# The experts' opening dealt into the last causal batch, weights cast midway, and the last batch routed one batch ahead

## Chip, cores and metric

The kernel runs on one core of one Trainium2 chip. The metric is the time of the device in microseconds (us). Several runs of a kernel give a median, and one more run is taken with the hardware profiler.

## What is computed

The input `x` has 8 batches of 512 positions with 512 channels. The reference applies three blocks, one after the other:

```python
x = x + tanh(g_xattn) * cross_attention(layernorm(x), ctx)     # pass A
y = layernorm(x)
y = y + latent_attention(rmsnorm(y, w_ln1))                    # pass B, causal, 16 heads
y = y + moe(rmsnorm(y, w_ln2))                                 # pass C
x = x + tanh(g_ffn) * y

def moe(x):
    shared = (silu(x @ sWg) * (x @ sWu)) @ sWd                 # one expert, all 4096 rows
    p = softmax(x @ Wgate + expert_bias)                       # 8 experts, the best 2 per row
    top_p, top_i = top_k(p, 2);  top_p /= sum(top_p)
    routed = sum_e comb[:, e] * ((silu(x @ Wg[e]) * (x @ Wu[e])) @ Wd[e])
    return shared + routed
```

The kernel computes `routed` only for the rows that chose an expert: it sorts them into 71 blocks of 128 rows, each with one expert.

## The kernel before

Every matrix product of pass C runs as three f16 products, from a high half (`_hi`, a cast) and a low half (`_lo`, the rest) of each operand. ACT writes the high halves, DVE or POOL the low ones.

**Order.** Each engine runs its own list of instructions in the order in which the Python code emits them, and they meet through semaphores. Passes A and B are generators with 64 steps for each batch, and `run_both` (L1615) deals B's first steps between A's last ones. B ends with an end body, which computes the last output projection. Its output `z` is stored to `z_all` by SP (L1111), POOL clears A's semaphores (L1218), and the block ends in a barrier (L1626). Pass C (`pass_c`, L1669) then begins with a block and memory of its own.

**Pass C, dense part.** It works on batches b = 0 to 7, and a body b does the shared expert of batch b and prepares batch b+1:

- SP loads `z` of a batch (1 MB, `load_z`, L1810) into one of four slots, and the f32 weights of one routed expert per body into a single stage (`gu_stage`, 1 MB in two transfers, L1819; `d_stage`, 0.5 MB, L1824). In a body's list stand, in this order, `load_z(b+3)` from body 1 to body 4, `up_weights(b+1)`, `down_weights(b+1)`. `load_z(b+3)` waits until the slot is free, which is when the store of batch b-1 has landed.
- POOL stores a finished batch with an accumulating transfer (`add_to_output`, L1878), so that of batch b-1 at the start of its body b. It also writes the routing records into a table with indirect transfers (`scatter`, L1901, 64 in all), takes the root for the norm (`rms`), and makes a low half (L1882).
- ACT squares and normalises the rows of batch b+2 (L2000, L2005), casts transposed rows (`high`, L1992), takes a tanh (`squash`, L2027), casts the hidden layer (`hidden_high`, L2033), scales by the gate (L2010) and casts the staged weights (`weights`, L2015 and L2017).
- DVE makes low halves (L2121, L2127, L2132), chooses the experts of a row (`choose`), works out its place in the table (`shares`, `read_ranks`, `place_rows`), makes the hidden layer (`activate`, L2277, L2280), and adds the gate and residual (`finish_rows`, L2290).
- PE, in a body: `up(b)` with 12 products to a chunk, four chunks (L2433 to L2435); four turns of batch b+1 (L2393); `route(b+1)` (L2403); `down(b)` (L2444 to L2446); `rank(b+1)` (L2416 to L2421), which ends the body. The last row of L2421 is used below as the mark of a body's end.

**Routed part.** After body 7 DVE lays out the blocks (`lay_starts`, `lay_blocks`). SP waits until all records are scattered, and loads the entries of each block (L1855). POOL gathers the rows of a block (L1948), ACT scales them, PE turns them (`x_turn`, L2485) and does up and down with that block's expert. POOL adds the result to the output in an indirect transfer. The gather of block 3 waits for all stores of the dense part. PE waits for the last casts and for the last dense output ahead of the loop.

## Time and profile before

| | |
|---|---|
| median of 3 runs | 2330.65 us (2325.38 to 2334.54) |
| the profiled run | 2325.74 us |
| its span | 2324.0 us, granted clock 0.964 |
| PE busy | 2103.3 us, 91% |
| DVE, ACT, POOL busy | 64%, 51%, 59% |

The times of the trace are us from the start of the span. Passes A and B take the stretch to about 1757, the dense part of C that from 1757 to 1963, and the routed blocks the rest. A row of the timeline gives the start, the length, the engine, the line and the operation, with the tile written ahead of the arrow, and in brackets how long the engine had been idle and what released it. A row marked x8 stands for eight instructions, and its time is that of the whole group. SPq rows are the moments at which SP issues a transfer, not the transfers.

### The profile page before, as it was taken

The numbers are of one execution on the slowest core, as the hardware profiler recorded it, in microseconds if no ns is written. First come the engines' busy times: TensorE is split into PE (matmuls) and PEld (weight loads), VectorE is DVE, ScalarE is ACT, GpSimd is POOL, SyncE is SP. The second block draws the span as 40 slices with busy tenths as digits, with TensorE's granted clock in tenths as the row PEclk, the third lists the DMA queues.
The fourth block names the chain that finished last, engine by engine and source line by source line (L and its number), as shares of the span: only waits on it lengthen the run. The fifth ranks groups of instructions, "written<-read, shape, count | busy, mean of one in ns | idle before, by whom it ended". The sixth has DMA issues, their size and how long they took to land. (4 is left out here: it accounts for less than half of the span.)

```text
span 2324.0 us, 43302 instructions
## 1 busy us (share of the span) xinstructions
PE 2103.3 (91%) x12568; PEld 958.9 (41%) x12569; DVE 1489.1 (64%) x4180; ACT 1180.0 (51%) x2319; POOL 1374.2 (59%) x1450
## 2 busy tenths in 40 slices
PE   2899999999999977799999999999984897899997
PEld 1333333333333312344444444544432443455554
DVE  3688888888888874466566565655544678344443
ACT  3355555555555544345545455554544673455554
POOL 4267776776776765255656565665661575455554
PEclk7999999999999987899999999999997998999999
DMA  5513323232332222534535354353514676666665
GB/s 161 168 55 110 101 85 103 81 115 73 107 97 92 78 98 86 170 115 139 159 118 153 117 163 134 114 174 98 155 49 159 120 156 126 114 116 112 115 109 91
DMA packets 227973, 272.15 MB, mean 117 GB/s; under 512 B 40152, under 2 KB 165964, under 8 KB 227508
## 3 DMA queue, kind: packets, MB, share of 16 engines
q1 hardware_dynamic: 197324, 212.76, 30.3%
q0 software_dynamic: 22752, 47.86, 12.1%
q10 hardware_dynamic: 7704, 9.20, 1.2%
q8 instruction: 92, 1.51, 0.3%
q14 instruction: 101, 0.83, 0.1%
HBM read 161.82 MB, written 86.54 MB: 107 GB/s over the span
## 5 line engine op out<-in xcount | busy, mean ns | idle before, releaser
L501 ACT ACTIVATE a_pt<-a_bank 128x512 f32<-128x512 f32 x512 | 305.6, 597 | 370.2 <-DVE a_bank L608 367.3
L1439 DVE CUSTOM_DVE_ANT_0 b_bank<-b_bank,b_tri 128x256 f32<-128x256 f32 (+3 forms) x512 | 253.2, 497 | 296.0 <-PE b_bank L1579 291.8
L619 DVE CUSTOM_DVE_ANT_0 a_bank<-a_bank,a_strip 128x512 f32<-128x512 f32 x512 | 353.2, 691 | 4.6 <-PE a_bank L762 3.9
L1192 POOL TENSOR_TENSOR b_acc<-b_acc,b_pt 128x256 f32<-128x256 f32 (+2 forms) x384 | 279.2, 749 | 84.2 <-ACT b_pt L1305 73.3
L411 POOL TENSOR_TENSOR a_acc<-a_acc,a_pt 128x512 f32<-128x512 f32 x256 | 317.5, 1271 | 16.2 <-ACT a_pt L501 15.7
L608 DVE TENSOR_TENSOR a_bank<-a_bank,a_band 128x256 f32<-128x256 f32 (+1 forms) x512 | 205.6, 402 | 129.7 <-PE a_bank L749 128.5
L1305 ACT ACTIVATE b_pt<-b_bank 128x256 f32<-128x256 f32 (+2 forms) x384 | 143.7, 383 | 187.1 <-PE b_bank L1563 171.1
L749 PE MATMUL a_bank<-a_q_stack,a_k_stack 128*128 128x512 f16 x512 | 199.2, 390 | 22.9 <-ACT a_pt L501 13.9
L762 PE MATMUL a_bank<-a_k_stack,a_q_stack 97*128 97x512 f16 x512 | 196.4, 384 | 3.6 <-DVE a_low L619 3.5
L1964 POOL DMA_INDIRECT out_dram<-c_z,c_to_row x71 | 112.5, 1585 | 133.8 <-DMA out_dram<-c_z,c_to_row 97.6
L1578 PE MATMUL b_bank<-b_k_stack,b_q_stack 96*128 96x256 f16 (+3 forms) x512 | 154.6, 302 | 16.0 <-DVE b_low L1439 8.7
L1561 PE MATMUL b_bank<-b_q_stack,b_k_stack 96*128 96x256 f16 (+3 forms) x512 | 156.4, 306 | 9.5 <-ACT b_pt L1305 5.6
L408 POOL TENSOR_TENSOR a_acc<-a_pt 128x512 f32<-128x512 f32 x128 | 159.9, 1269 | 4.9 <-ACT a_pt L501 4.9
L429 POOL TENSOR_TENSOR a_o_un<-a_o_un,a_den 128x512 f32<-128x512 f32 x32 | 41.3, 1292 | 204.4 <-DVE a_den L572 204.4
L1563 PE MATMUL b_bank<-b_q_stack,b_k_stack 97*128 97x256 f16 (+3 forms) x512 | 154.2, 301 | 0.0
L1579 PE MATMUL b_bank<-b_k_stack,b_q_stack 96*128 96x256 f16 (+3 forms) x512 | 153.2, 300 | 0.0
L777 PE MATMUL a_bank<-a_pt,a_v 128*32 128x512 f32 x1024 | 142.4, 629 | 1.1 <-ACT a_pt L501 1.1
L1207 POOL TENSOR_TENSOR b_o_un<-b_o_un,b_den 128x512 f32<-128x512 f32 x32 | 40.8, 1276 | 157.1 <-DVE b_den L1395 147.3
L749 PEld LDWEIGHTS a_bank<-a_q_stack,a_k_stack 128*128 128x128 f16 x512 | 49.5, 97 | 183.0 <-ACT a_pt L501 91.1
L1305 ACT ACTIVATE b_acc<-b_bank 128x512 f32<-128x512 f32 x128 | 74.7, 596 | 92.4 <-PE b_bank L1563 86.4
L1562 PE MATMUL b_bank<-b_hidden,b_far 128*128 128x128 bf16 x512 | 113.0, 221 | 0.0
L2343 DVE TENSOR_TENSOR c_xt_lo<-c_bank,c_xt_hi 128x512 f16<-128x512 f32 x71 | 49.0, 691 | 94.3 <-ACT c_xt_hi L2082 94.3
(338 smaller groups left out, 5352.7 us busy)
## 6 DMA issues: line engine op xcount, KB each, us to landing
b_q_stack<-qk_rows SPq DMA_DIRECT2D x192, 128.0 KB, 2.6
a_q_stack<-qk_rows SPq DMA_DIRECT2D x96, 128.0 KB
a_k_stack<-qk_rows SPq DMA_DIRECT2D x96, 128.0 KB
b_k_stack<-qk_rows SPq DMA_DIRECT2D x96, 128.0 KB, 2.6
a_sums<-in_x SPq DMA_DIRECT2D x34, 256.0 KB, 3.2
qk_rows<-a_qk_hi SPq DMA_DIRECT2D x64, 128.0 KB, 1.7
qk_rows<-a_qk_lo SPq DMA_DIRECT2D x64, 128.0 KB, 1.8
out_dram<-a_sums SPq DMA_DIRECT2D x32, 256.0 KB, 2.0
```

Source lines behind the costliest of these rows:

```text
L408: nc.gpsimd.tensor_tensor(acc[:, hh, :], pt[:, (n - HG) % SLOTS, :], mine, ALU.add).then_inc(pooled, 1)
L411: nc.gpsimd.tensor_tensor(acc[:, hh, :], acc[:, hh, :], mine, ALU.add).then_inc(pooled, 1)
L501: nc.scalar.activation(pt[:, n % SLOTS, :], st_bank[n % 2][:], ACT.Exp).then_inc(exped, 1)
L608: nc.vector.tensor_tensor(st_bank[n % 2][:, c0:c1], st_bank[n % 2][:, c0:c1], band[:, h, at:at + c1 - c0], ALU.add).then_inc(biased, 1)
L619: nc.vector.tensor_tensor_reduce(out=max_bank[step % 2][:], in0=max_bank[step % 2][:], in1=strip[:, g * HG + hh, at:at + S], scale=-1.0, s ...
L749: mm(st_bank[n % 2][:], k_stack[:, h, j * P:(j + 1) * P], q_stack[:, h, :], start=True, stop=True).then_inc(scored, 1)
L762: mm(max_bank[step % 2][:], q_stack[0:MASK + 1, h, i * P:(i + 1) * P], k_stack[0:MASK + 1, h, :], start=True, stop=True).then_inc(maxed, 1)
L1192: nc.gpsimd.tensor_tensor(sums_of, sums_of, probs(n), ALU.add).then_inc(pooled, 1)
L1305: nc.scalar.activation(probs(n), st_bank[n % 2][:, 0:w], ACT.Exp).then_inc(exped, 1)
L1439: nc.vector.tensor_tensor_reduce(out=max_bank[step % 2][:, 0:w], in0=max_bank[step % 2][:, 0:w], in1=tri[:, at:at + w], scale=-1.0, scalar ...
L1561: mm(o, k_stack[0][0:LOW, h, j * P:(j + 1) * P], q_stack[0][0:LOW, h, j * P:], start=True, stop=False)
L1578: mm(o, q_stack[0][0:LOW, h, c], k_stack[0][0:LOW, h, 0:w], start=True, stop=False)
```

## The change

Lines of the changed kernel are those of its own file.

1. **One program.** `run_all` takes the place of `run_both` and of C's own block. C's passes become generators too. C's opening (all that PE, ACT, DVE and POOL do ahead of body 0, with `up(0, 0, 0)`) is cut into 90 steps, and these are dealt between B's steps from step 38 of B's last batch. `inputs_used` (B's last query and key rows are consumed) and `all_used` (B's last output is evicted) are the waits that stand in place of the barrier.
2. **Memory.** C's tiles and PSUM banks are laid over what B has finished with. The shared expert's halves get tiles of their own (`own_gu_hi` and others), and C uses B's identity matrix.
3. **SP.** C's constants, z(0), the shared expert's weights, z(1) and the blank table are issued in B's last batch, ahead of its last four stores. z(2) and z(3) follow after B's end.
4. **Semaphores.** POOL clears A's semaphores at the start of B's third batch instead of at B's end.
5. **Weights cast midway.** ACT's cast of the next expert's up weights moves from the end of body b to its middle, between `high(b+1, 1)` and `high(b+1, 2)`; the cast of the down weights to behind `hidden_high(b, 1)`. DVE makes the low halves of the same expert in the same body, where it made them one body later before.
6. **Last batch ahead.** Batch 7 is routed within body 6. POOL has 3 of the 32 row tiles to scatter in body 7, where it had 4. DVE lays out the blocks at the start of body 7, and takes the first three `from_row` there. PE turns block 0 ahead of its waits for casts and output.

The core of the diff:

```diff
 JOIN = 46
+NEXT_JOIN = 38
+OPENING = 2 * UNITS - NEXT_JOIN
@@ pass B, SP body
+                if kind == "last":
+                    yield
@@ run_both -> run_all
+    def chained(second, third):
+        for at, _ in enumerate(second):
+            if at >= next_joined:
+                next(third)
+            yield
+        yield from third
@@ pass C, SP
-            sp.dma_start(table, blank_rows).then_inc(blanked, 16)
-            load_z(0)
+            prior.inputs_used(sp)
...
+            load_z(0)
             sp.dma_start(r_stage[:], ...)
             up_weights(0)
             down_weights(0)
             load_z(1)
+            sp.dma_start(table, blank_rows).then_inc(blanked, 16)
+            yield
+            prior.all_used(sp)
             load_z(2)
+            sp.wait_ge(prior.z1_stored, 64 * B + 16)
             load_z(3)
             for b in range(B):
...
                 if b and b + 3 < B:
                     load_z(b + 3)
                 up_weights(b + 1)
                 down_weights(b + 1)
@@ pass C, ACT
-            square(0)
...
+            for s in range(OPENING):
+                if s < NT:
+                    square(0, (s,))
...
+                if 8 <= s < 8 + NT:
+                    normalise(0, (s - 8,))
+                if 12 <= s < 12 + NK:
+                    up_weights(0, (s - 12,))
...
+                yield
+            prior.all_used(act)
             for b in range(B):
                 more = b + 1 < B
                 squash(b, 0)
                 if more:
                     high(b + 1, 0)
                     high(b + 1, 1)
-                    scale_gate(b + 1, range(0, 2))
+                up_weights(b + 1)
+                if more:
                     high(b + 1, 2)
                     high(b + 1, 3)
                 hidden_high(b, 0)
                 if b + 2 < B:
                     square(b + 2)
                 squash(b, 1)
                 if more:
-                    scale_gate(b + 1, range(2, 4))
+                    scale_gate(b + 1, range(0, 2))
+                if b + 2 == B:
+                    exponential(b + 1)
                 hidden_high(b, 1)
+                down_weights(b + 1)
                 if b + 2 < B:
                     normalise(b + 2)
+                    exponential(b + 1)
                 if more:
-                    exponential(b + 1)
-                weights(b + 1)
+                    scale_gate(b + 1, range(2, 4))
@@ pass C, PE
+            for s in range(OPENING):
+                if 13 <= s < 13 + NT:
+                    turn(0, s - 13)
+                if s == 40:
+                    route(0)
+                    up(0, 0, 0)
+                yield
+            prior.all_used(pe)
             for b in range(B):
-                up(b, 0, 0)
-                if b == 0:
+                more, early = b + 1 < B, b + 2 == B
+                if b:
+                    up(b, 0, 0)
+                else:
                     rank(0)
...
                 up(b, 1, 0)
+                if early:
+                    route(b + 1)
                 up(b, 1, 1)
-                if more:
+                if more and not early:
                     route(b + 1)
                 for t in range(NT - 1):
                     down(b, t, (0,))
+                if early:
+                    rank(b + 1)
```

On ACT, in the body of batch 1 of the dense part (`c_th` is `squash`, `c_xt_hi` is `high`, `c_h_hi` is `hidden_high`, the squares write `c_xn,c_squares`), the order before was:

```order
L2027 ACTIVATE c_th<-c_bank 128x512 [waits c_half_done,c_up_done]
L1992 ACTIVATE c_xt_hi<-c_bank 128x4x128 [waits c_logits_done,c_up_done,c_turned] x2
L2010 ACTIVATE c_z<-c_z,c_gate 128x512 [waits c_xn_ready]
L2010 ACTIVATE c_z<-c_z,c_gate 128x512
L1992 ACTIVATE c_xt_hi<-c_bank 128x4x128 [waits c_logits_done,c_up_done,c_turned] x2
L2033 ACTIVATE c_h_hi<-c_hid 128x512 [waits c_downed,c_hidden]
L2000 ACTIVATE c_xn,c_squares<-c_z 128x512 [waits c_turned,c_z_loaded0]
```

and it is now, with the body's second half:

```order
L2099 ACTIVATE c_th<-c_bank 128x512 [waits c_half_done,c_up_done]
L2062 ACTIVATE c_xt_hi<-c_bank 128x4x128 [waits c_logits_done,c_up_done,c_turned] x2
L2085 ACTIVATE c_gu_hi<-c_gu_stage,c_wn 128x512 [waits c_gu_loaded]
L2085 ACTIVATE c_gu_hi<-c_gu_stage,c_wn 128x512 x3
L2062 ACTIVATE c_xt_hi<-c_bank 128x4x128 [waits c_logits_done,c_up_done,c_turned] x2
L2105 ACTIVATE c_h_hi<-c_hid 128x512 [waits c_downed,c_hidden]
L2070 ACTIVATE c_xn,c_squares<-c_z 128x512 [waits c_turned,c_z_loaded3]
L2070 ACTIVATE c_xn,c_squares<-c_z 128x512 x3
L2099 ACTIVATE c_th<-c_bank 128x512 [waits c_half_done,c_up_done]
```

The cast of the staged weights, which waits for their load, now stands between the two pairs of `high`; before, it stood behind the body's last instructions.

On SP, the loads of the dense part's bodies 0 to 2 in the changed kernel (L1867 is `load_z`, L1876 the up weights, L1881 the down weights, L1904 a part of the table):

```order
L1876 DMA c_gu_stage<-in_Wg 128x4x256 [waits c_w_split]
L1876 DMA c_gu_stage<-in_Wu 128x4x256
L1881 DMA c_d_stage<-in_Wd 128x2x512 [waits c_w_split]
L1904 DMA table<-c_blank 128x8x4 [waits a_m_stacked1,a_m_stacked2]
L1867 DMA c_z<-z_all 128x4x512 [waits c_out_stored0]
L1876 DMA c_gu_stage<-in_Wg 128x4x256 [waits c_w_split]
L1876 DMA c_gu_stage<-in_Wu 128x4x256
L1881 DMA c_d_stage<-in_Wd 128x2x512 [waits c_w_split]
L1867 DMA c_z<-z_all 128x4x512 [waits c_out_stored1]
L1876 DMA c_gu_stage<-in_Wg 128x4x256 [waits c_w_split]
```

Nothing moved here: the same rows, with the waits of the same semaphores, stand in the same order in the kernel before.

On PE, at the end of pass B, the last rows of its output projection and the first of pass C before:

```order
L1483 MATMUL b_bank<-b_wo_hi,b_o_hi 128x512 [waits b_o_lo_done]
L1484 MATMUL b_bank<-b_wo_lo,b_o_hi 128x512
L1485 MATMUL b_bank<-b_wo_hi,b_o_lo 128x512
L1626 UNCONDITIONAL_BRANCH
L2382 UNCONDITIONAL_BRANCH [waits barrier_Pool_Activation_PE_DVE_SP_release]
L2393 MATMUL c_bank<-c_idn,c_xn 128x128 [waits c_xn_ready,c_const_set,c_const_loaded]
```

and now, from the end of C's first chunk of `up` (L2539 to L2541) and from the end of the output projection (L1498 to L1500) on:

```order
L2539 MATMUL c_bank<-c_xt_hi,c_own_gu_hi 128x512
L2540 MATMUL c_bank<-c_xt_lo,c_own_gu_hi 128x512
L2541 MATMUL c_bank<-c_xt_hi,c_own_gu_lo 128x512
L1498 MATMUL b_bank<-b_wo_hi,b_o_hi 128x512 [waits b_o_lo_done]
...
L1500 MATMUL b_bank<-b_wo_hi,b_o_lo 128x512
L2522 MATMUL c_bank<-c_chosen,c_before_p 128x32 [waits a_normed,c_const_set,b_left_dve]
```

The turns, `route(0)` and the first `up` stand ahead of B's last chains, and `rank(0)` is the first of C's rows behind them.

## Rows read from the trace of the kernel before

**Rows 1.** The page: busy tenths of PE in 40 slices of the span.

```profile
PE   2899999999999977799999999999984897899997
```

**Rows 2.** Busy us by stretch: PE, PEld, DVE, ACT, POOL; clock, DMA share, GB/s.

```profile
1690.00:1741.50 51.50, 44.41 (x352) 19.96 (x350) 20.08 (x67) 26.23 (x62) 32.68 (x44) 0.97 0.15 50
...
1757.00:1789.00 32.00, 9.86 (x82) 6.57 (x83) 9.71 (x36) 19.29 (x44) 4.93 (x19) 0.57 0.77 262
...
1812.50:1904.50 92.00, 80.58 (x581) 42.37 (x579) 68.17 (x209) 60.92 (x120) 60.41 (x65) 0.94 0.80 157
1904.50:1943.50 39.00, 37.75 (x295) 20.40 (x293) 34.62 (x105) 23.87 (x45) 29.58 (x32) 1.00 0.76 136
```

**Rows 3.** Timeline, all engines: from B's last product to C's first rank.

```profile
1755.00 0.38 PE L1485 MATMUL b_bank<-b_wo_hi,b_o_lo 128*128 128x512 f16 x1
...
1766.03 0.63 ACT L2000 ACTIVATE c_xn<-c_z 128x512 f32<-128x512 f32 x1 [19.55 <-DMA c_z<-z_all]
...
1770.97 1.94 PE L2393 MATMUL c_bank<-c_idn,c_xn 128*128 128x128 f32 x8 [15.59 <-ACT c_xn L2005]
...
1788.96 0.24 PE L2421 MATMUL c_bank<-c_chosen,c_ones 128*128 128x8 f16 x4
```

**Rows 4.** Timeline of PE: ends of bodies 0, 1, 2 and 6.

```profile
1812.48 0.24 PE L2421 MATMUL c_bank<-c_chosen,c_ones 128*128 128x8 f16 x4
...
1831.78 0.24 PE L2421 MATMUL c_bank<-c_chosen,c_ones 128*128 128x8 f16 x4
...
1859.75 0.24 PE L2421 MATMUL c_bank<-c_chosen,c_ones 128*128 128x8 f16 x4
...
1943.47 0.24 PE L2421 MATMUL c_bank<-c_chosen,c_ones 128*128 128x8 f16 x4
```

**Rows 5.** Timeline, bodies 1 to 4: stores, SP's next loads, ACT's casts of them.

```profile
1813.24 1.41 POOL L1878 DMA_DIRECT2D out_dram<-c_z  x1 [4.57 <-DVE c_z L2290]
...
1827.24 0.37 SPq L1810 DMA_DIRECT2D c_z<-z_all  x1
...
1838.54 1.46 POOL L1878 DMA_DIRECT2D out_dram<-c_z  x1
...
1849.93 0.37 SPq L1810 DMA_DIRECT2D c_z<-z_all  x1
...
1850.64 0.37 SPq L1819 DMA_DIRECT2D c_gu_stage<-in_Wg  x1
...
1859.19 2.56 ACT L2015 ACTIVATE c_gu_hi<-c_gu_stage,c_wn 128x512 f16<-128x512 f32 x4 [1.59 <-DMA c_gu_stage<-in_Wu]
...
1873.75 0.51 SPq L1819 DMA_DIRECT2D c_gu_stage<-in_Wg  x1
...
1884.17 2.56 ACT L2015 ACTIVATE c_gu_hi<-c_gu_stage,c_wn 128x512 f16<-128x512 f32 x4 [7.26 <-DMA c_gu_stage<-in_Wu]
```

**Rows 6.** SP's waits by cause, 1757 to 1960: total us, times, longest.

```profile
SPq L1810 <- DMA out_dram<-c_z: 46.5, 3, 19.4
```

**Rows 7.** Transfers: number, size, median us from issue to landing.

```profile
out_dram<-c_z POOLq DMA_DIRECT2D x8, 1024.0 KB, 11.2
...
c_gu_stage<-in_Wu SPq DMA_DIRECT2D x8, 512.0 KB, 6.9
```

**Rows 8.** Timeline: a stall of PE in body 2; second tanh and end of body 3.

```profile
1843.74 1.94 PE L2393 MATMUL c_bank<-c_idn,c_xn 128*128 128x128 f32 x8 [5.65 <-DVE c_xt_lo L2121]
...
1870.64 0.57 ACT L2027 ACTIVATE c_th<-c_bank 128x512 f32<-128x512 f32 x1
...
1879.06 0.24 PE L2421 MATMUL c_bank<-c_chosen,c_ones 128*128 128x8 f16 x4
```

**Rows 9.** Timeline behind body 7: first turn, gather of block 3, its turn.

```profile
1976.68 1.97 PE L2485 MATMUL c_bank<-c_idn,c_z 128*128 128x128 f32 x8 [13.24 <-ACT c_z L2077]
...
1985.72 1.06 POOL L1948 DMA_INDIRECT c_z<-z_all,c_from_row  x1 [9.05 <-DMA out_dram<-c_z]
...
1992.14 0.60 PE L2485 MATMUL c_bank<-c_idn,c_z 128*128 128x128 f32 x4
```

429 lines of the change are left out of this document (254 added, 175 removed).

## The prediction

> **What bounds the kernel now.** I read the page first: PE is busy nine tenths of the span and has one long dip near three quarters of it, and one short dip after that [rows 1]. Any gain or loss lies there. The windows then cut that part into stages [rows 2]. In the tail of pass B (1690 to 1741.5) PE is busy 44.41 of 51.5 us beside ACT's 26.23 and POOL's 32.68. In C's opening (1757 to 1789) it is busy 9.86 of 32, at a granted clock of 0.57, while ACT works 19.29. Bodies 1 to 4 of the dense part (1812.5 to 1904.5) take 92 us, with PE busy 80.58; bodies 5 and 6 take 39, with PE busy 37.75. A body without a disturbance is thus 19.5 us long, and PE's products set it.
>
> The timeline shows what the opening costs: the last output product is at 1755.00, ACT's first square at 1766.03, after 19.55 us idle for `z` to come back from memory, the first turn at 1770.97, and `rank(0)` ends the opening at 1788.96 [rows 3]. Bodies 0, 1 and 2 then end at 1812.48, 1831.78 and 1859.75: 23.5, 19.3 and 28.0 us [rows 4].
>
> Last I followed the weights. In bodies 1 to 4 SP issues `load_z(b+3)`, and behind it the weights for the next cast. SP's wait for the slot, that is for POOL's accumulating store, is the cause of 46.5 us of SP's idle time [rows 6]. The store of body 1 is issued at 1813.24 and SP goes on at 1827.24, 14.0 us later; in body 2 it is 1838.54 and 1849.93, 11.4 us [rows 5]. Then the weights are issued, and ACT's cast of them starts 8.5 us later (1850.64 to 1859.19), in the next body 10.4 us later (1873.75 to 1884.17), both times after a wait for that load [rows 5]. So the weights of body 2 are cast at 1859.19, when PE has all but finished body 2 (1859.75). In the kernel before this lateness is nearly free, since the cast is the last thing on ACT's list for that body, and what is cast is used only in the routed part.
>
> **The change, part by part.** I sum against the profiled run, 2325.74 us, which lies 4.9 us below the median of three.
>
> *Join: -24.* What is removed is the way from B's last product to `rank(0)`, 1755.0 to 1789.0, 34 us [rows 3]. Back come two things. First, `route(0)` and the first `up` must still run on PE, some 3.8 us (an estimate: 48 narrow and 12 wide products, the wide ones 0.38 us long with about half of it overlapped [rows 3]); they stand ahead of B's last output chain, in a tail where PE is idle 7.1 of 51.5 us [rows 2], so I count half of it, 2. Second, B's tail grows. ACT gets nearly all of the 19.29 us that it works in the opening [rows 2] added to the tail, where it had 25.3 us free in 51.5; POOL gets the two norm roots. ACT and PE wait for each other there at each step, so free time is not fully usable. Below it costs 0, if all fits between; above 12, if 60% of ACT's work lengthens the tail. I take 7, nearer to the upper half because ACT would be 88% busy (45.5 of 51.5). `rank(0)` then comes near 1765: 24 saved, between 18 and 31.
>
> *Early loads, memory, semaphores: 0.* SP's loads go out in the last batch, where the DMA share is 0.15 [rows 2], and POOL's 64 clears move to a place where POOL waits for others. If a load should be late for the opening, it costs what the join gains, and that lies in its range.
>
> *Body 0: +2.5.* z(2), z(3) and the first expert's weights, 3 MB, can only start after B's last store; the cast now stands in the middle of body 0. With some 2 us until the store has landed, 10 for the loads (the slower of [rows 5] is 10.4) and 14 or 15 from the cast to the body's end (next paragraph) it takes 26 us, and took 23.5 [rows 3, 4].
>
> *Cast in the middle, bodies 1 to 4: +64.* This adds a wait to ACT, and its list goes on behind that wait: `high(b+1, 2)` and `high(b+1, 3)`, without which PE can't `route`; then `hidden_high(b, 0)`, without which PE can't `down`; then the squares, the second tanh, the second `hidden_high`. PE, DVE and POOL all stop there. SP's order has not been changed: `load_z(b+3)`, which waits for the store of batch b-1, stands ahead of the weights for this cast. And that store is only issued after body b-1 has ended. So within one body there is now a chain with nothing to hide it: end of body b-1, store, `z` load issued, weights loaded, cast, second half of the body. Its pieces:
>
> - end of the body to store: 0.8 us in body 1 (1812.48 to 1813.24), 6.8 in body 2, where POOL still has scatters queued (1831.78 to 1838.54) [rows 4, 5]; I take 2 each for bodies 3 and 4, together 11.6;
> - store to SP's next issue: 11.4 (14.0 in body 1, whose store ran beside other loads) [rows 5], four times 45.6;
> - from there to the issue of the weights 0.7, and to the cast 9.0, between the 8.5 and 10.4 of [rows 5]: 38.8;
> - cast 2.56 [rows 5], then two `high`, one `hidden_high` and four squares, seven operations of the size of one of the cast's four (0.6 each, 4.2), so 6.7 until the second tanh; from there to the end of the body 8.4 (1870.64 to 1879.06 in body 3) [rows 8]: 15.1, four times 60.4.
>
> Together 156.4, where the four took 92.0: +64. The lower bound takes the median landings, 11.2 and 6.9 [rows 7], stores issued at once and 13 for the last piece: 4 x 32.3 = 129, +37. For the upper bound, PE stands still some 15 us in each body. In the trace a PE that had stood for 15.59 us was granted 0.57 over the stretch [rows 2, 3], nearer to the lower of its two levels (1.2 of 2.4 GHz). Then the fifteen last products take twice as long, some 3 us more a body, and with loads of 10.4 the sum is 174, +82.
>
> What the row shows of the store is 11.2 us from issue to landing for 1 MB [rows 7]. The Trainium skill, page "DMA: Bandwidth & Descriptors", section "Anatomy of one DMA — SWDGE (gpsimd) path", gives a fit of 2.0 us and bytes over 436e3 per us, by which 1 MB would be an estimated 4.4 us; four bodies would then be 27 us shorter and the whole near 2333. The trace doesn't agree for this accumulating store, and the row decides. The same section says that a DMA engine does not wait on semaphores, and that the wait is on the issuing sequencer; SP's 46.5 us [rows 6] agree.
>
> *Bodies 5 and 6: +2.* No `z` is loaded there, so the weights come a body ahead: 0. Batch 7's choice and places run within body 6, where DVE already works 34.62 of 39 in two bodies [rows 2]; I give 2, between 0 and 4.
>
> *Last batch ahead: -10.* From body 6's end to the turn of block 3 it took 48.7 us (1943.47 to 1992.14) [rows 4, 9]. With the table laid out early, the first gathers no longer lie behind the dense part's end, and PE's 13.24 us of idle ahead of its first turn go. Next is the gather of block 3, which waits for the last store: body 7's products, 19.5 as in bodies 5 and 6 [rows 2], finishing 1, store 11.2 [rows 7], gather to turn 6.4 (1985.72 to 1992.14) [rows 9], together 38.1. The bounds are -6, if the entries come late, and -14, if the store is 3 or 4 us shorter.
>
> Sum: -24 + 2.5 + 64 + 2 - 10 = +34.5, so 2360 us.
>
> **Rivals.**
>
> *Hidden after all: faster.* The weights land before ACT comes to the cast, because the store is issued earlier or SP's wait is met sooner than I think. Bodies 1 to 4 then take 4 x 19.3 = 77 [rows 4], 15 less than now, and body 0 its +2.5: 2325.7 - 24 + 2.5 - 15 + 2 - 10 = 2281. Against it: even in the kernel before, ACT waited for this load at the body's very end [rows 5]. This side begins when the four bodies take under 28.6 us on average: gains and losses are level at (92.0 + 24 - 2.5 - 2 + 10) / 4 = 30.4 us each. I give 0.12.
>
> *Level: within 0.5%.* The chain is there, but its transfers are shorter, since they run more by themselves (the same bytes at a DMA share of 0.80 in 92 us [rows 2] would be some 0.5 in 150). With 9.5 for the store, 6.9 for the load [rows 7], 13 for the tail and stores issued after 1 us, a body is 30.8 us: 2327. Against it: the store of body 2 had no `z` or up weights beside it and still took 11.4 [rows 5]. 0.14. The shorter store that the Trainium skill's fit gives would fall on this side too.
>
> *Join lost as well: slower still.* ACT's added work lengthens B's tail by its whole 19 us and the opening's own chain is stretched; -24 becomes -10, and the time 2374. For it: the 88% on ACT. Against it: of the idle time in the opening, 15.59 us is PE's wait for a load, a norm and ACT [rows 3], which is gone either way. 0.10.
>
> *My forecast*, 2342 to 2370: 0.64.
>
> **How the numbers follow.** About 0.5% is what a measurement of this kernel can tell from no change, here 2319 to 2342 around the median. Slower takes the forecast and the lost join: 0.74; the same 0.14; faster 0.12. The predicted time is the forecast's, 2360. The range of 8 in 10 runs from 2332, inside the level case, to 2380, the upper bound of the chain with a good join; it leaves out the faster case, part of the level one, and little above.
>
> **What the profile of the changed kernel would show.** Join right: the first `up` products ahead of B's last output products, no gap of 15 us between the two passes, `rank(0)` near 1765. Chain right: ACT's cast of `c_gu_hi` waits for the transfer into `c_gu_stage` some 10 to 18 us in each of four bodies, PE idles ahead of `route` or `down`, its granted clock falls in these bodies, and they are 36 to 42 us long; SP's wait on the store still stands ahead. Last batch right: the turn of block 3 about 38 us after body 6's end. Wrong would be: casts of bodies 1 to 4 with short waits and ends 19 to 25 us apart (faster), or a B tail that ends much after 1765.

## The result and the profile after

The changed kernel takes 2378.98 us (median of four runs, 2375.21 to 2381.74), beside 2328.30 for the kernel before: 1.0213 times as long, 95% interval 1.0186 to 1.0240. Its profiled run is one of 2375.21 us with a span of 2373.4, so 49.4 us of span came on top; the forecast was 34.5. The page of the profile shows where: PE's dip near three quarters of [rows 1], one deep slice, has become a trough over four slices, and in three of them the granted clock is at 7 tenths (in one before).

```profile
PE   2899999999999968899999999999976658899997
PEclk8999999999999978999999999999987779899999
```

The windows of the changed kernel, in the columns of [rows 2]: the tail of pass B with the opening dealt into it, the stretch from there to `rank(0)`, bodies 1 to 4, and about bodies 5 and 6.

```profile
1690.00:1757.00 67.00, 53.91 (x383) 24.02 (x381) 32.97 (x83) 44.40 (x106) 38.48 (x61) 0.86 0.32 105
1757.00:1772.70 15.70, 14.13 (x107) 6.64 (x106) 5.68 (x25) 0.95 (x3) 2.49 (x3) 0.96 0.14 51
1801.00:1954.00 153.00, 88.45 (x602) 44.59 (x601) 69.32 (x210) 60.67 (x121) 60.01 (x65) 0.75 0.51 105
1954.00:1988.70 34.70, 34.25 (x277) 18.86 (x274) 30.16 (x100) 22.80 (x44) 26.13 (x29) 1.00 0.73 124
```

PE does in 153 us what took it 92: 88.45 us busy beside 80.58 before, and 64.6 us idle beside 11.4. The granted clock of 0.75 lies between the two levels (1.2 and 2.4 GHz); before it was 0.94. The timeline of PE gives the marks: the last product of B, `rank(0)`, and the ends of bodies 0 to 4.

```profile
1771.46 0.38 PE L1500 MATMUL b_bank<-b_wo_hi,b_o_lo 128*128 128x512 f16 x1
1772.74 0.24 PE L2527 MATMUL c_bank<-c_chosen,c_ones 128*128 128x8 f16 x4
1801.42 0.24 PE L2527 MATMUL c_bank<-c_chosen,c_ones 128*128 128x8 f16 x4
1841.04 0.24 PE L2527 MATMUL c_bank<-c_chosen,c_ones 128*128 128x8 f16 x4
1882.66 0.24 PE L2527 MATMUL c_bank<-c_chosen,c_ones 128*128 128x8 f16 x4
1917.30 0.24 PE L2527 MATMUL c_bank<-c_chosen,c_ones 128*128 128x8 f16 x4
1953.89 0.24 PE L2527 MATMUL c_bank<-c_chosen,c_ones 128*128 128x8 f16 x4
```

Against [rows 3, 4], `rank(0)` is 16.2 us earlier, body 0 takes 28.7 us and not 23.5, bodies 1 to 4 take 39.6, 41.6, 34.6 and 36.6 (152.5 together, and not 92.0). The waits between 1774 and 1960, by engine, name one transfer and what stands behind it (total us, times, longest):

```profile
SPq L1867 <- DMA out_dram<-c_z: 119.0, 4, 38.3
ACT c_gu_hi L2085 <- DMA c_gu_stage<-in_Wu: 85.1, 5, 20.9
PE c_bank L2509 <- DVE c_xt_lo L2212: 54.8, 5, 16.2
```

SP's wait for the store was 46.5 us in [rows 6]. The timeline of body 2 shows the links: the store of body 1, SP's load of `z` and of the weights, ACT's cast in the middle of the body, PE's `route`, ACT's second tanh.

```profile
1846.42 1.47 POOL L1939 DMA_DIRECT2D out_dram<-c_z  x1
...
1857.11 0.37 SPq L1867 DMA_DIRECT2D c_z<-z_all  x1
1857.52 0.51 SPq L1876 DMA_DIRECT2D c_gu_stage<-in_Wg  x1
...
1866.41 2.56 ACT L2085 ACTIVATE c_gu_hi<-c_gu_stage,c_wn 128x512 f16<-128x512 f32 x4 [20.91 <-DMA c_gu_stage<-in_Wu]
...
1870.23 0.19 PE L2509 MATMUL c_bank<-c_r_hi,c_xt_hi 128*128 128x8 f16 x1 [16.24 <-DVE c_xt_lo L2212]
...
1872.80 0.58 ACT L2099 ACTIVATE c_th<-c_bank 128x512 f32<-128x512 f32 x1
```

The end of the dense part: the last store, the gather of block 3 and its turn.

```profile
2022.20 1.44 POOL L1939 DMA_DIRECT2D out_dram<-c_z  x1 [2.12 <-DVE c_z L2382]
2032.52 1.06 POOL L2022 DMA_INDIRECT c_z<-z_all,c_from_row  x1 [8.88 <-DMA out_dram<-c_z]
...
2040.03 1.06 PE L2608 MATMUL c_bank<-b_idn,c_z 128*128 128x128 f32 x4
```

Body 6's last output product begins at 1994.9; from its end to this turn it is 45 us, where [rows 4, 9] had 48.7.

### The profile page after: what moved, and what is told of

Its sections match the earlier page's. It is cut to its first block, busy times and chain, and to the rows that moved or that the text cites. A ratio compares the mean times of both kernels' runs of the same rounds, so it can differ in the third digit from the quotient of the medians.

```text
span 2373.4 us, 43310 instructions
## 1 busy us (share of the span) xinstructions
PE 2118.2 (89%) x12568; PEld 960.9 (40%) x12569; DVE 1494.6 (63%) x4180; ACT 1179.5 (50%) x2319; POOL 1374.3 (58%) x1450
## 4 chain that ended last, share of the span: by engine, by line
PE 61%; DMA 14%; DVE 8%; issue 6%; POOL 5%; ACT 4%; SPq 2%; ACTq 0%; POOLq 0%; DVEq 0%
PE a_bank L700 12%; DMA out_dram<-c_z,c_to_row 5%; PE a_bank L780 5%; PE a_bank L752 4%; PE b_bank L1498 4%; PE a_bank L765 4%; PE b_bank L1499 4%; PE b_bank L1500 4%; PE b_bank L1578 2%; DMA out_dram<-c_z 2%; PE b_bank L1610 2%; PE b_bank L1595 2%; PE b_bank L1596 2%; PE b_bank L1580 2%; DMA c_gu_stage<-in_Wu 2%
## 5 line engine op out<-in xcount | busy, mean ns | idle before, releaser
L414 POOL TENSOR_TENSOR a_acc<-a_acc,a_pt 128x512 f32<-128x512 f32 x256 | 317.5, 1271 | 16.2 <-ACT a_pt L504 15.7
L752 PE MATMUL a_bank<-a_q_stack,a_k_stack 128*128 128x512 f16 x512 | 199.4, 390 | 22.8 <-ACT a_pt L504 13.9
L2618 PE MATMUL c_bank<-c_gu_hi,c_xt_hi 128*128 x284 | 108.9, 383 | 0.0
```

The lines of the kernel that those rows point to most:

```text
L414: nc.gpsimd.tensor_tensor(acc[:, hh, :], acc[:, hh, :], mine, ALU.add).then_inc(pooled, 1)
L752: mm(st_bank[n % 2][:], k_stack[:, h, j * P:(j + 1) * P], q_stack[:, h, :], start=True, stop=True).then_inc(scored, 1)
```

## The experiments

All of them compute the whole reference. The table has, from each profiled run, the marks used so far. Starts drift by some us between runs of one kernel, so `rank(0)` is also given as the time from ACT's copy `b_m_row` in B's last batch to it ("tail"); the work that the opening adds between B's steps on ACT stands nearly all behind this copy. All columns but the first are single traces.

| kernel | median us | tail | body 0 | bodies 1 to 4 | body 5 | end of body 5 to turn of block 3 |
|---|---|---|---|---|---|---|
| before | 2328.3 | 83.8 | 23.5 | 92.0 | 19.3 | 68.3 |
| after | 2379.0 | 66.9 | 28.7 | 152.5 | 19.3 | 66.8 |
| before, casts midway | 2381.8 | no join | 23.5 | 150.3 | 20.1 | 64.8 |
| after, weights ahead of `z` | 2319.5 | 69.1 | 30.3 | 96.5 | 19.9 | 65.3 |
| after, casts at the end | 2314.0 | 66.5 | 24.1 | 91.3 | 25.3 | 67.4 |
| after, weights one body ahead | 2299.8 | 68.2 | 24.0 | 84.9 | 20.6 | 67.0 |
| that, without early routing | 2296.1 | 68.6 | 24.2 | 84.0 | 20.3 | 65.9 |
| that, tail, scatters, store | 2297.3 | 62.7 | 24.3 | 85.4 | 19.3 | 65.3 |
| tail, thinner scatters | 2293.0 | 61.3 | 24.4 | 81.4 | 19.3 | 66.4 |
| that, weights two ahead | 2287.4 | 64.8 | 23.9 | 77.2 | 19.3 | 66.4 |

**The cast in the middle, alone.** In the kernel before only the two casts and DVE's low halves are moved.

```diff
+                up_weights(b + 1)
                 if more:
                     high(b + 1, 2)
...
                 hidden_high(b, 1)
+                down_weights(b + 1)
...
-                weights(b + 1)
```

> The kernel before with one edit: the casts of the routed weights in the middle of a body and DVE's low halves in the same body, as in the change; no join, no early routing. Theory A: the four bodies grow by 55 to 65 us and the time goes from about 2327 to about 2387. Theory C (it takes the join or the new layout): within 5 us of 2327.

Measured: 1.0232 times the kernel before (1.0207 to 1.0258), bodies 1 to 4 in 150.3 us, without join, early routing or new memory. The waits on ACT and SP are the two of the changed kernel:

```profile
ACT c_gu_hi L2015 <- DMA c_gu_stage<-in_Wu: 64.1, 4, 19.2
...
SPq L1810 <- DMA out_dram<-c_z: 116.2, 4, 38.2
```

So the cast's place by itself makes the loss: bodies 1 to 4 are 58 us longer than before, where the changed kernel's are 60. Body 0 stays at 23.5 here, since z(2), z(3) and the weights are under way before the dense part begins.

**The casts back at the end.** The opposite: the changed kernel with both casts, and DVE's low halves, where they were before.

```diff
-                up_weights(b + 1)
...
-                down_weights(b + 1)
...
                     scale_gate(b + 1, range(2, 4))
+                up_weights(b + 1)
+                down_weights(b + 1)
```

> The changed kernel with ACT's casts of the routed weights put back to the end of a body and DVE's low halves one body later, as in the kernel before; the join and the routing of the last batch stay. Theory A: the late weights hold up nothing that PE needs, so bodies 1 to 4 take 90 to 100 us again and the time is about 2318. Theory C (the new memory layout or the join itself made the bodies long): they stay near 150 and the time near 2376.

Measured: 0.9935 (0.9913 to 0.9956), bodies 0 to 5 at 24.1 and 91.3 and 25.3. The loss is gone, and body 0's 5 us too. What is left is a gain of 14 us, less than the join's, and body 5, with 25.3 us and not 19.3, takes 6 of it back.

**The cast midway, SP's order turned round.** One step in SP's list of the changed kernel:

```diff
-                if b and b + 3 < B:
-                    load_z(b + 3)
                 up_weights(b + 1)
                 down_weights(b + 1)
+                if b and b + 3 < B:
+                    load_z(b + 3)
```

> The changed kernel with one edit: in SP's list of a body the two loads of weights stand ahead of load_z(b+3), not behind it. Theory A (the chain through SP's order: store, z load, weights, cast): bodies 1 to 4, which took 152.5 us in the changed kernel, fall to 80 to 90 (body 1 still waits for the blank table's issue ahead of its weights), ACT's wait on the staged up weights falls from 85 us to under 30, and the time from about 2376 to about 2310. Theory B (the cast in the middle is itself too much for ACT or the queues are full, whatever SP's order): bodies stay above 33 us each and the time above 2360.

Measured: 0.9959 (0.9943 to 0.9974). The cast stays midway and nothing is removed, yet 56 of the 60 us are gone: the cast isn't dear, but what SP has to issue ahead of its weights. The four bodies take 96.5 us, more than the 80 to 90 that were expected. Body 1 is still 31.7 us long (1803.88 to 1835.53): ACT's cast waits 12.69 us there. The first weights can't go out before B's end, and the next, issued at 1805.97 and 1806.60 behind a part of the blank table, take 12.9 and 14.4 us to land beside the store of body 0.

**And the first weights before B's end.** SP issues the first routed expert's weights in B's last batch, and each later pair one body ahead.

```diff
             yield
+            up_weights(1)
+            down_weights(1)
+            yield
             prior.all_used(sp)
...
             for b in range(B):
+                if b:
+                    up_weights(b + 1)
+                    down_weights(b + 1)
...
-                up_weights(b + 1)
-                down_weights(b + 1)
```

> The changed kernel with SP's loads of weights ahead of load_z and of the blank table in every body, and those for body 0 issued ahead of the end of pass B. Theory A: bodies 0 to 4 take 19 to 21 us each, against 28.7 and four of 38 in the changed kernel, so 80 to 85 us less: about 2293. Rival: z now comes late, ACT waits for it at the squares and gives back 10 us or more, so about 2305 or above.

Measured: 0.9870 (0.9844 to 0.9897). ACT's waits for weights come to 3.0 us in all. The time is 7 us above the forecast 2293, since not all bodies reach the 19 to 21 us expected: body 0 is back at 24.0, as before the change, and body 2 takes 26.0, where bodies 1, 3 and 4 take 19.3 to 20.3. In body 2 POOL is late, not a load:

```profile
1823.23 1.46 POOL L1944 DMA_DIRECT2D out_dram<-c_z  x1
...
1836.08 1.14 POOL L1948 TENSOR_TENSOR c_h_lo<-c_hid,c_h_hi 128x512 f16<-128x512 f32 x1
1837.37 0.59 PE L2555 MATMUL c_bank<-c_own_d_hi,c_h_hi 128*128 128x512 f16 x1 [3.87 <-POOL c_h_lo L1948]
```

POOL has eight scatters of body 1 to issue, some 1.3 us each, until 1823.2, 7 us into body 2, and its six of body 2 ahead of the norm's root.

**What lengthens the tail of B.** Three runs single out a suspect each, all on the kernel with the early weights, one run of each. First 2 MB of the loads are held back until the stores of B's last batch have been issued, because the first exponential of that batch comes 6.92 us behind `b_m_row` in the changed kernel and 4.45 in the one before.

```diff
             up_weights(0)
+            yield
             down_weights(0)
             load_z(1)
             sp.dma_start(table, blank_rows).then_inc(blanked, 16)
-            yield
```

> The kernel e7_weights_early, in which SP holds back the shared down weights, z(1) and the blank table (2 MB) until the four stores of the last causal batch are issued. In the changed kernel the last batch's small row of maxima, issued by ACT at 1706.1, is waited for by PE until 1712.0 (2.3 us idle), right behind 3 MB of C's loads. Theory A (these loads delay it): that wait goes, and rank(0) comes 2 to 3.5 us earlier than 1772.9. Theory B (the wait has another cause, or ACT's work is late anyway): rank(0) within 1 us of 1772.9.

Measured: 2298.34 us, tail 67.0, and the exponential still 6.58 us behind the copy. `rank(0)` comes 2.0 us earlier, as the first theory had it, but 0.7 of that is the start's drift, and the wait that the theory named has hardly shrunk. So these 2 MB are at most a small part of it. PE waits there for the transfer of `b_m_row` (4 KB): from issue to landing it took 3.0 us in the kernel before, 5.9 in the changed one, and 5.5 with the early weights, whether the 2 MB are held back or not. The shared up weights still land beside it here, until 1709.04, and B's four stores now stand where the held loads stood. Whether these make it late was not tried, so the cause of the 2.4 us stays open.

Second, ACT's gate scaling and second normalise moved behind B's last exponential:

```diff
-                if 18 <= s < 18 + NT:
-                    scale_gate(0, (s - 18,))
...
-                if 30 <= s < 30 + NT:
-                    normalise(1, (s - 30,))
                 if s == 42:
                     exponential(0)
+                if 43 <= s < 43 + NT:
+                    scale_gate(0, (s - 43,))
+                if 47 <= s < 47 + NT:
+                    normalise(1, (s - 47,))
```

> The kernel e7_weights_early, with two of the opening's pieces on ACT, scale_gate(0) (four operations, 2.9 us) and normalise(1) (four, 2.6 us, and a wait of 2.4 us for POOL's root), moved behind the last exponential of pass B, where ACT waits anyway. Theory A (each operation put between B's steps lengthens the tail by its own time, though ACT is idle a third of it): the last exponentials and rank(0) come 5 to 7 us earlier than 1772.9. Theory B (ACT's free time takes the operations in, and only the wait for POOL counts): 2 to 3.5 us earlier. Theory C (PE or DVE sets the tail): within 1 us.

Measured: 2299.99 us, tail 66.5. ACT's last exponential is 5.8 us earlier than with the early weights alone, and the tail only 1.7, since PE then waits for POOL:

```profile
1752.97 1.94 PE L1532 MATMUL b_bank<-b_acc,b_ones_f 128*32 128x512 f32 x8 [5.07 <-POOL b_acc L1206]
```

Third, beside that, POOL's second root for the norm moved behind its last add of B (`if s == 27:` to `if s == 44:`).

> The kernel e9_act_out_of_tail with one more move: POOL's second norm root (rms(1), 1.2 us) behind pass B's last adds. In e9 the last exponential came 5.8 us earlier than in e7_weights_early, but PE then waited 5.07 us for POOL's last add. Theory P (POOL sets the tail): from the last row of maxima to rank(0) 65.0 to 65.5 us, 1.0 to 1.5 less than e9's 66.5. Rival (PE or the output chain): within 0.5 us of e9.

Measured: 2304.69 us, tail 68.8: no gain in the whole, which is inconclusive, since in this one run the stretch ahead of POOL's part is 3.9 us longer than in the run before it. In POOL's part, from its second-last scaling `b_o_un` to its last add, it takes 13.3 us, beside 14.65 in the changed kernel and 10.6 before. So the root, 1.3 us, is a third of the difference.

The rest shows when rows of both engines are laid side by side. DVE and POOL in the changed kernel:

```profile
1739.30 5.21 DVE L2219 SCALAR_TENSOR_TENSOR c_own_gu_lo<-c_gu_stage,c_wn,c_own_gu_hi 128x512 f16<-128x512 f32 x4
1741.11 4.26 POOL L1205 TENSOR_TENSOR b_acc<-b_acc,b_pt 128x384 f32<-128x384 f32 x3
1744.43 2.02 DVE L2225 SCALAR_TENSOR_TENSOR c_own_d_lo<-c_d_stage,c_own_d_hi 128x1024 f16<-128x1024 f32 x1
1745.34 2.13 POOL L1223 TENSOR_TENSOR b_o_lo<-b_o_un,b_o_hi 128x512 f16<-128x512 f32 x1
```

and the same operations in the kernel before, where POOL's were in B's tail and DVE's in the opening:

```profile
1732.12 2.90 POOL L1192 TENSOR_TENSOR b_acc<-b_acc,b_pt 128x384 f32<-128x384 f32 x3
1734.99 1.14 POOL L1210 TENSOR_TENSOR b_o_lo<-b_o_un,b_o_hi 128x512 f16<-128x512 f32 x1
...
1780.62 2.73 DVE L2127 SCALAR_TENSOR_TENSOR c_gu_lo<-c_gu_stage,c_wn,c_gu_hi 128x512 f16<-128x512 f32 x4
1783.27 1.22 DVE L2132 SCALAR_TENSOR_TENSOR c_d_lo<-c_d_stage,c_d_hi 128x1024 f16<-128x1024 f32 x1
```

Each is 1.5 to 1.9 times as long when the other runs. POOL's rows and its scaling ahead of them (1.61 beside 1.27 us) are 2.7 us longer together, the other two thirds of the difference.

**Tail, scatters and store together.** On the version without early routing (below): ACT's and POOL's moves of the last two runs, DVE's low halves of the shared expert four steps earlier, where POOL is mostly idle; two row tiles scattered in the middle of body 1, so that fewer pile up; the last store ahead of the first gathers.

```diff
-                if 19 <= s < 19 + NK:
-                    up_weights(0, (s - 19,))
-                if s == 23:
+                    up_weights(0, (s - 15,))
+                if s == 19:
...
-                if b > 1:
-                    scatter_some(b, 1)
+                if b:
+                    scatter_some(b, 1 if b > 1 else 2)
```

> The kernel e11_no_early_route with these moves: in pass B's tail, ACT's scale_gate(0) and normalise(1) and POOL's second norm root (rms(1)) come behind the last exponential, and DVE makes the low halves of the shared weights four to eight steps earlier, when POOL is idle; in body 1 POOL scatters two tiles between its two low halves and two behind them, not four behind; the last store goes ahead of the first three gathers. Theory P (POOL's adds, made longer by its own new work and by DVE running beside it, set B's tail): from the last row of maxima on ACT to rank(0) it takes 62 to 64 us, against 66.9 in the changed kernel and 66.5 in e9_act_out_of_tail. Rival (PE's own order, with route and up ahead of the last output chain, sets it): 66 or more. Body 2 falls from 26 to about 20 us if the queue of scatters on POOL made it long, and the turn of block 3 comes 3 to 4 us sooner. Sum: about 2283, against 2296.1 for e11 in one run.

Measured: 0.9869 (0.9842 to 0.9896), a median of 2297.28 us where 2283 was expected, and no better than without the three. The tail does shrink, to 62.7, and POOL's adds and low half are back at their old lengths:

```profile
1732.40 0.74 DVE L2220 SCALAR_TENSOR_TENSOR c_own_gu_lo<-c_gu_stage,c_wn,c_own_gu_hi 128x512 f16<-128x512 f32 x1
...
1741.94 2.91 POOL L1206 TENSOR_TENSOR b_acc<-b_acc,b_pt 128x384 f32<-128x384 f32 x3
1744.81 1.16 POOL L1224 TENSOR_TENSOR b_o_lo<-b_o_un,b_o_hi 128x512 f16<-128x512 f32 x1
```

But body 1 takes 27.2 us and body 2 19.3: the stall has only moved. The first scatter waits for the blank table, and `c_h_lo` stands behind four scatters.

```profile
1806.70 1.12 POOL L1967 DMA_INDIRECT table<-c_record,c_place_i  x1 [3.04 <-DMA table<-c_blank]
...
1815.02 0.58 PE L2551 MATMUL c_bank<-c_own_d_hi,c_h_hi 128*128 128x512 f16 x1 [5.62 <-POOL c_h_lo L1948]
```

The store's place gains 0.6 us at most: it goes out 43.5 us after body 5's end, not 47.3, but the first gathers now follow behind it, and PE idles 15.01 us ahead of its first turn.

**The last batch ahead, undone.** The version with the early weights, with batch 7 routed in body 7 as before.

```diff
-                more, early = b + 1 < B, b + 2 == B
+                more, early = b + 1 < B, False
...
-                known = B if b >= B - 2 else b + 1
+                known = b + 1
```

> The kernel e7_weights_early without the routing of the last batch one batch ahead: batch 7 is routed in body 7, its blocks are laid out behind the second activate, and from_row is taken behind finish_rows, as in the kernel before. From the end of body 5 to the turn of block 3 it took 68.3 us in the kernel before, and 67.0 in e7. Theory A (the early routing gains about 10 us and loses them by the order behind body 7): 64 to 66 us here, as in the kernel before with casts in the middle (64.8). Theory B (the early routing is worth what I forecast and something else was lost): 72 us or more.

Measured: 2296.12 us (one run), 65.9 us from the end of body 5 to the turn of block 3, beside 67.0 with early routing. This part of the change gains nothing here.

**DVE's work behind body 7 in another order.** With early routing kept, the layout of the blocks moved behind the first `activate` of body 7, the third `from_row` behind `finish_rows`, and the third gather behind the store.

```diff
                     lay_starts()
-                    lay_blocks()
...
                     low_part(0)
+                    lay_blocks()
```

> The kernel e7_weights_early, with DVE's lay_blocks behind the first activate of body 7, its third from_row behind finish_rows, and POOL's third gather behind the last store. In the changed kernel finish_rows of batch 7 stood behind the third from_row, which waited for its entry, and the last store came 27 us after the body began. Theory A (the waits put ahead of finish_rows took the gain of the early routing): the store goes 4 to 6 us earlier, and from the end of body 5 to the turn of block 3 it takes 61 to 63 us, not 67.0. Theory B (entries or gathers set the turn): within 1.5 us of 67.

Measured: 2306.35 us, 68.1 us for that stretch. A miss: the layout, 5 us of DVE's time in a row, now delays the second `activate` instead of the first, and PE waits 6.39 us for `c_h_lo` where it had waited 3.25.

**Thinner scatters.** The tail's edits kept, gathers ahead of the store again, three row tiles in body 1 and three in body 2.

```diff
-                if b > 1:
+                if b > 2:
                     scatter_some(b, 2)
...
-                if b:
-                    scatter_some(b, 1 if b > 1 else 2)
+                if b > 1:
+                    scatter_some(b, 1)
...
-                    scatter_some(b, 2)
+                    scatter_some(b, 2 if b > 1 else 3)
```

> The version of the run without early routing, with the tail's edits of the combined run (gate scaling, second normalise and second root behind the tail, DVE's low halves earlier), the first gathers again ahead of the last store, and a thinner start of the scatters: 3 row tiles at the end of body 1 (4 before), 3 in body 2 (5 before), 5 in each later one, so 6 are left for body 7 (4 before), where POOL stood idle 8.85 us. Theory (the combined run lost its gain to POOL's backlog in body 1, and the end gains nothing by the store's place): from the last row of the causal batch's sums to rank(0) 62 to 65 us, bodies 1 and 2 19.3 and 19.5 to 21.5 us instead of 46.5 together in the combined run, end of body 5 to the turn of block 3 65 to 68; span 2287 to 2290. Rival (a stall of some 6.5 us comes somewhere in bodies 1 and 2 whatever POOL does, for instance from the loads): bodies 1 and 2 together stay at 45 to 47, span about 2295.

Measured: 0.9854 (0.9836 to 0.9872); tail 61.3, bodies 1 and 2 both 19.3 us. The theory holds for these bodies, but body 3 now takes 23.5 us, which it had not foreseen, and the span of 2290.7 ends just above its 2287 to 2290. There the old chain is seen again: the weights stand behind the load of `z`, and this behind the store.

```profile
1826.98 0.37 SPq L1868 DMA_DIRECT2D c_z<-z_all  x1
1827.40 0.51 SPq L1877 DMA_DIRECT2D c_gu_stage<-in_Wg  x1
...
1837.11 2.56 ACT L2088 ACTIVATE c_gu_hi<-c_gu_stage,c_wn 128x512 f16<-128x512 f32 x4 [2.82 <-DMA c_gu_stage<-in_Wu]
```

**Weights two ahead.** So SP issues each pair of weights ahead of one more load of `z`.

```diff
             for b in range(B):
-                if b:
-                    up_weights(b + 1)
-                    down_weights(b + 1)
                 if b == 1:
+                    up_weights(2)
+                    down_weights(2)
...
+                if b and b + 2 <= B:
+                    up_weights(b + 2)
+                    down_weights(b + 2)
                 if b and b + 3 < B:
                     load_z(b + 3)
```

> The run with the thinner start of the scatters, and in SP's list each expert's weights stand one load of z earlier: the weights for the cast of body b+1 are issued in body b ahead of load_z(b+3), not behind it. In the run before this, body 3 took 23.5 us: the store of body 1 went out at 1815.07, SP's load of z behind it at 1826.98, the weights of body 3 right behind that, and ACT's cast waited 2.82 us and started 4 us later in its body than in bodies 1 and 2. Theory (body 3 is the last remnant of the same chain through SP's list): the weights of body 3 are issued when DVE's low halves of the expert before are done, near 1823, no cast waits for a load, body 3 takes 19.3 to 20 us, span 2286 to 2288. Rival (the store sets it by another way, the load of z(5), now some 2 us later, and the squares behind it): body 3 stays at 22 to 25 us with ACT waiting for z, span 2289 to 2293.

Measured: 2287.40 us (five runs), 0.9837 (0.9814 to 0.9860). Each of bodies 1 to 5 takes 19.3 us, here the ends of bodies 1, 3 and 4, and the window of bodies 1 to 4:

```profile
1814.54 0.24 PE L2530 MATMUL c_bank<-c_chosen,c_ones 128*128 128x8 f16 x4
...
1853.15 0.24 PE L2530 MATMUL c_bank<-c_chosen,c_ones 128*128 128x8 f16 x4
1872.45 0.24 PE L2530 MATMUL c_bank<-c_chosen,c_ones 128*128 128x8 f16 x4
...
1795.30:1872.50 77.20, 75.41 (x582) 40.75 (x579) 67.46 (x209) 60.56 (x120) 54.22 (x59) 1.00 0.89 177
```

PE is busy 75.41 of 77.2 us at the full granted clock, with the cast still midway. This is the best version found: 38 us below the kernel before as measured beside it (2325.2), 92 below the changed one. The five spans run from 2284.6 to 2291.8, the last of which is the profiled one; their median, 2285.6, lies just below the forecast 2286 to 2288.

## Why the prediction was right, and where it was not

The direction and its cause were right: 2360 was forecast, slower, and 2379 came, inside the range by 1 us. The sum was 19 us short of the median. Against the profiled runs, as the prediction summed, it is 15 us (49.4 of span against 34.5). The upper end of the range was built on a longer chain with a good join. It was reached another way: the chain came out 4 us shorter than forecast, and the join, body 0 and the last batch missed by 7.8, 2.7 and 6.3 us. That the time still fell inside is luck in part. The five terms as measured below add up to 48 us; another 1.5 lie behind the turn of block 3 (333.4 us to the end, 331.9 before).

**Cast in the middle: right.** Forecast +64 (156.4 us for four bodies), measured +60.4 (152.5). Its pieces over the four bodies: end of the body to the store 9.1 (forecast 11.6), store to SP's next issue 46.2 (45.6), from there to the cast 35.7 (38.8), cast to the body's end 61.5 (60.4). The run with only the casts moved shows it alone (150.3), and the run with only SP's order turned round takes it away (96.5) with the cast still there. So the price is that of the place in SP's list, as the prediction argued.

One reading in it was off: the lateness was not "nearly free" in the kernel before. The second cast of [rows 5] starts 5.1 us behind body 3's end (1879.06 [rows 8]), and body 1's own cast as far behind body 1's end:

```profile
1836.83 2.56 ACT L2015 ACTIVATE c_gu_hi<-c_gu_stage,c_wn 128x512 f16<-128x512 f32 x4 [7.20 <-DMA c_gu_stage<-in_Wu]
```

ACT's `high` of the next body stands behind it, PE then waits for `c_xt_lo` (5.65 us in body 2 [rows 8], 3.75 in body 4), and these are the two long bodies, of 28.0 and 25.5 us. By these rows some 15 of the 92 us were in the chain already, and came back in full only in the last version, with 77.2. In [rows 1] the prediction also passed over the dip in slices 15 to 17, which is over well before the opening begins.

Between the two prices of the store the prediction went by the row, 11.2 us [rows 7], and that was right. In the changed kernel five such stores between 1774 and 1960 take 11.0 us in the median, in a stretch where the DMA share was only 0.51. The rival "level", in which the transfers shorten because they run more by themselves, falls with the same figure. The Trainium skill's fit (page "DMA: Bandwidth & Descriptors", section "Anatomy of one DMA — SWDGE (gpsimd) path") would make it an estimated 4.4 us for 1 MB; the trace doesn't agree for this accumulating store.

**Join: the term that was mis-sized.** Forecast -24, measured -16.2, or -16.8 from `b_m_row`. What was removed was as forecast: from B's last product to `rank(0)` 34.0 us before, 1.3 now. What came back was put at 9 and is 15.9, so the saving lies below the 18 to 31 that was given for it. Three stretches of the tail carry it. From `b_m_row` to POOL's second-last `b_o_un` it is 33.7 us (25.7 before), 8 more, of which 2.5 is the open wait for `b_m_row`'s transfer. From there to POOL's last add it is 14.65 (10.6), 4 more. From there to B's last product it is 17.3 (13.5), 3.7 more.

`route(0)` and the first `up` were put at 2, half of their 3.8 us, and that came true by luck in part, since the half was taken from PE's idle time over the whole window and not from the place. They ran from 1760.44 to 1764.24, where PE in the kernel before had waited 1.76 us for POOL's low half, so 2 us were left. The other 1.9 of the 3.7 us is PE's clock. Here are the sums' products and the wait in the kernel before, then the same products in the changed one:

```profile
1741.60 1.07 PE L1516 MATMUL b_bank<-b_acc,b_ones_f 128*32 128x512 f32 x8 [2.93 <-POOL b_acc L1192]
...
1747.77 0.39 PE L1483 MATMUL b_bank<-b_wo_hi,b_o_hi 128*128 128x512 f16 x1 [1.76 <-POOL b_o_lo L1210]
```

```profile
1754.34 1.93 PE L1531 MATMUL b_bank<-b_acc,b_ones_f 128*32 128x512 f32 x8 [0.87 <-POOL b_acc L1205]
```

From 1736 to 1754 PE was busy 13.3 of 18 us at a granted clock of 0.69, and from 1754.3 to 1758.3 it was granted 0.51, the lower level; from 1758.3 on it had 1.00 again. In the two last versions the same products stand at the same place, the clock is 1.00 from the sums' products on, and the stretch is 15.4 us, 1.9 more than before the change.

The step that was mis-sized is "I take 7, nearer to the upper half because ACT would be 88% busy": 7 us for the growth of the tail apart from these products, and it is 13.9. The argument looked at ACT alone and gave POOL two norm roots. It did not weigh DVE's low halves against POOL's adds beside them, which with the second root make the 4 us of the second stretch, nor the clock. With ACT's and POOL's moves and DVE's low halves earlier, the three last versions have tails of 62.7, 61.3 and 64.8, 5 us under the 67.9 of the six runs with the same opening (66.5 to 69.1); their second stretch is 11.2 to 11.5 us.

Of the first stretch's 8 us, 5.5 are not explained by any run. ACT was busy 26.0 of 33.7 us there (14.74 of 25.7 before), as the prediction feared, but moving eight of its operations away took it from 35.0 (early weights alone) only to 33.3, and in the three last versions it is 33.2, 33.2 and 36.7. That ACT's remaining work sets it is argued, not shown.

"Early loads, memory, semaphores: 0" may have failed too: the transfer of `b_m_row` took 5.9 us and not 3.0 in the stretch where the early loads were under way, but the run that held 2 MB of them back hardly changed it.

**Body 0: half of it missed.** Forecast +2.5, measured +5.2. From the cast to the body's end it took 14.8 us, as forecast (14 to 15); from `rank(0)` to the cast it took 13.8, where 12 had been put for the landing of the store and the loads. With the weights issued ahead of B's end the body takes 24.0, so it was these loads.

**Bodies 5 and 6: right.** Forecast +2, measured +2.2, all of it in body 6.

**Last batch ahead: wrong, and for a reason the forecast had not seen.** Forecast -10, measured -3.7. The step that failed is "body 7's products, 19.5, finishing 1": the last store goes out 27 us after body 6's end, not 20.5. PE stands 3.26 us behind DVE in body 7, which lays out the blocks there, and the last products end 23 us after body 6's. From there to the store it is 3.6 us more: DVE's third `from_row` waits 2.96 us for its entry, and the finish of all four row tiles stands behind it. And the gain isn't the early routing's: with it undone the stretch from body 5's end is 65.9 us beside 67.0, and in the kernel before with only the casts moved it is 64.8 beside 68.3. The rows of DVE and POOL in the kernel before suggest what the casts have to do with it:

```profile
1966.96 2.73 DVE L2127 SCALAR_TENSOR_TENSOR c_gu_lo<-c_gu_stage,c_wn,c_gu_hi 128x512 f16<-128x512 f32 x4
1969.60 1.22 DVE L2132 SCALAR_TENSOR_TENSOR c_d_lo<-c_d_stage,c_d_hi 128x1024 f16<-128x1024 f32 x1
...
1971.68 0.99 POOL L1948 DMA_INDIRECT c_z<-z_all,c_from_row  x1 [12.64 <-DVE c_from_row L2348]
...
1975.19 1.48 POOL L1878 DMA_DIRECT2D out_dram<-c_z  x1
```

DVE's low halves of the last expert stood behind the last rows' finish and ahead of the `from_row` for which the first gather waits, and the last store stood behind the gathers. With casts and low halves midway those 3.9 us are out of that chain, about the 3.5 that the run with only the casts moved gained there. The prediction had not followed DVE's part of the moved cast to the end.

**The rivals.** "Hidden after all" foresaw bodies 1 to 4 in 77 us if the weights came in time. They didn't in the changed kernel. In the last version they do, at 77.2 us; the whole is then 2287, though with other edits in the tail and without the early routing. "Join lost as well", at 2374 the rival nearest to the result, was met in its first half: 7.8 of its 14 us were lost.

**The sums.** Three of them don't add up as they stand, and none changes the side of the forecast. For the join, 34 less 2 and 7 is 25, and 24 was taken. The lower bound's pieces (11.2, 6.9, 13) come to 31.1 us a body, or 31.8 with the 0.7 to the issue, and not 32.3. Those of "level" (9.5, 6.9, 13, 1) come to 30.4, or 31.1, and not 30.8.

## To carry to other kernels

When a consumer is moved forward, look at what its producer's issue stands behind on the issuing engine: here one load of `z` ahead of the weights, which had cost some 15 us in four bodies while the cast was the last thing in a body, cost 60 more once it wasn't, and moving two issues gave 56 of these back. When work is dealt into a busy tail, price each piece on the engine and at the place where it will stand, and look at which engine is next in line there: a wait at that very place took in half of PE's added work here, while POOL and DVE, left out of the price, slowed each other. After each stall removed, read the trace again for the next: here the loads, then POOL's scatters, then the loads once more.

## What had not been expected of the hardware

DVE and POOL slowed each other. DVE's 128x512 low half with two operands in SBUF took 0.68 us (2.73 for four) when POOL was nearly idle and 1.30 (5.21 for four) beside POOL's 128x384 adds, which themselves took 1.42 instead of 0.97; POOL's 128x512 low half took 2.13 instead of 1.14 beside DVE's 128x1024 one, which took 2.02 instead of 1.22. Moved to where POOL is mostly idle, they were back at 0.74 (one by itself) and 1.18 for DVE, 0.97 and 1.16 for POOL; only POOL's scaling, which started beside DVE's 128x1024 half, still took 1.86 instead of 1.27. The Trainium skill's page "SBUF — State Buffer", section "Who interferes with whom", says that a DVE instruction with two SBUF inputs contends with a GpSimd instruction that reads SBUF, and calls the ports that they share an exclusive lock. The trace agrees that they contend. It does not show that one waits until the other is through: alone DVE's four low halves and POOL's scaling and three adds take 2.73, 1.27 and 2.90 us, 6.9 in a row, and they were done in 6.1 (1739.30 to 1745.37), with the first 0.9 us of DVE's next low half besides.
